# Graph attention as one loop per layer with a running softmax, in place of three stages

## The chip, the cores and the metric

The kernel runs on one core of a Trainium2 chip. The metric is the device time of one execution in microseconds. The core has five engines that run side by side, each through its own instruction queue: TensorE (PE), VectorE (DVE), ScalarE (ACT), GpSimd (POOL) and SyncE (SP). PE writes to eight PSUM banks; everything else lies in SBUF or in DRAM. SP and POOL start the DMAs here, POOL the indirect ones (gathers and scatters by a list of rows). Engines wait for each other only by semaphores.

## The reference

Eight layers, four graph layers and four mixtures of experts, on 3125 nodes of 256 numbers and 50000 edges sorted by destination. The change touches only the third graph layer, a graph attention of two layers with 8 heads of 32:

```python
q = (h @ Wq).reshape(n, H, DK)
k = (h @ Wk).reshape(n, H, DK)
v = (h @ Wv).reshape(n, H, DV)
e = jnp.sum(q[dst] * k[src], axis=-1) / np.sqrt(DK).astype(np.float32)
m = jax.ops.segment_max(e, dst, num_segments=n)
a = jnp.exp(e - m[dst])
z = jax.ops.segment_sum(a, dst, num_segments=n)
alpha = a / (z[dst] + 1e-09)
msg = v[src] * alpha[:, :, None]
agg = jax.ops.segment_sum(msg, dst, num_segments=n).reshape(n, H * DV)
out = agg @ Wo
return _layer_norm(out + h, g, b)
```

## The kernel before

Nodes stand in NT = 25 tiles of 128 rows. The edges are sorted by destination and cut into CHUNKS = 416 chunks of 128, so that all edges of a chunk have their destination in one tile; `chunks.bin` holds each chunk's tile. A step of the attention's loops takes GS = 4 chunks, so there are 104 steps. All matmuls are fp32, which PE runs in two passes: a matmul counts as two in the profile.

`layer2_gnn` runs for each of its two layers: `dense` (q into SBUF, k and v side by side into the DRAM table `pairs`), then three stages, one after the other with a barrier between, and then the division by z, the product with Wo and the layer norm.

`attention_scores`: POOL gathers rows of k and v, 128 rows of 2 KB for each chunk, into a ring `rows` of 16 chunks (L1000). SP writes the v half of each group of 4 chunks to the DRAM buffer `spill` (L1865, 512 KB). DVE builds one-hot matrices of the destination lanes (L1836), PE turns them (L1901), ACT copies them to SBUF (L1921), PE picks with them each edge's q row (L1909). For each chunk PE first loads the number of its tile from SBUF into a register (L1908). DVE multiplies q and k (L1882) and sums over each head (L1888). A slot of the ring comes free when its reduction and its spill are done. A loop over registers (`steps`) repeats a body of four steps.

`attention_weights`: with all scores there, they are turned to lie by head, and DVE runs scans over 3328 columns forward and back (L2069, L2082, L2084) that give each edge the maximum of its destination; small products of 16 columns carry maxima from block to block. ACT takes the exponential, and all is turned back.

`attention_values`: SP reads `spill` back, DVE builds the same one-hots again (L1836) and multiplies v by the weights (L2132), POOL puts the weights beside them as a count column (L2144), PE sums each chunk into the PSUM bank of its tile (L2162, 264 columns), tiles going round over 8 banks. When a tile has ended, ACT copies its bank to `acc` (L2178) and clears it (L2180).

## Time and profile before

| | us |
|---|---|
| median of 3 runs | 7547.13 |
| lowest and highest | 7526.02, 7561.16 |
| span of the profiled execution | 7555.1 |
| scores stage, layers one and two | 743.4, 746.6 |
| weights stage | 63.4, 63.7 |
| values stage | 200.8, 201.4 |

The page gives the profiled execution by its span alone, from the first instruction to the last. Busy time over the whole program is an average over very different stages (PE 67%, DVE 38%, POOL 29%), and says little on the attention. A stretch of time with the busy time of each engine in it says more. "issue" beside idle time means that the engine waited for nothing that the profile shows. The names of some releasers (`home_rows`, `bias`) are those of other stages that used the same semaphore.

### The profile page before, as it was taken

The numbers are of one execution on the slowest core, as the hardware profiler recorded it, in microseconds if no ns is written. First come the engines' busy times: TensorE is split into PE (matmuls) and PEld (weight loads), VectorE is DVE, ScalarE is ACT, GpSimd is POOL, SyncE is SP. The second block draws the span as 40 slices with busy tenths as digits, with TensorE's granted clock in tenths as the row PEclk, the third lists the DMA queues.
The fourth block names the chain that finished last, engine by engine and source line by source line (L and its number), as shares of the span: only waits on it lengthen the run. The fifth ranks groups of instructions, "written<-read, shape, count | busy, mean of one in ns | idle before, by whom it ended". The sixth has DMA issues, their size and how long they took to land. (4 is left out here: it accounts for less than half of the span.)

```text
span 7555.1 us, 86117 instructions
## 1 busy us (share of the span) xinstructions
PE 5066.7 (67%) x21628; PEld 3356.8 (44%) x21677; DVE 2842.8 (38%) x6162; ACT 1117.7 (15%) x2691; POOL 2221.8 (29%) x2417
## 2 busy tenths in 40 slices
PE   3511969659783597755454965554877969898954
PEld 2410547314771256733222843222767844444433
DVE  4260679201323004244445944445943220202052
ACT  2210235000220002210000120000123220101020
POOL 3356010540244401425553215553300410000014
PEclk9999999769796697977776976777988989999966
DMA  0000023223561223637774827675721644243323
GB/s 14 1 1 1 1 93 139 81 66 120 160 199 65 77 90 123 195 122 228 219 218 137 273 86 224 216 222 160 254 67 40 191 153 153 101 139 115 115 69 114
DMA packets 484296, 952.76 MB, mean 126 GB/s; under 512 B 112617, under 2 KB 292436, under 8 KB 481686
## 3 DMA queue, kind: packets, MB, share of 16 engines
q1 hardware_dynamic: 324614, 633.98, 24.9%
q0 software_dynamic: 114208, 281.05, 12.8%
q10 hardware_dynamic: 45296, 35.56, 1.6%
q8 instruction: 88, 1.44, 0.1%
q14 instruction: 90, 0.74, 0.0%
HBM read 733.91 MB, written 216.46 MB: 126 GB/s over the span
## 5 line engine op out<-in xcount | busy, mean ns | idle before, releaser
L1173 PE MATMUL banks<-ring,xn 128*128 128x512 f32 (+1 forms) x3500 | 1443.9, 568 | 397.6 <-issue 276.9
L1173 PEld LDWEIGHTS banks<-ring,xn 128*128 128x128 f32 x3500 | 644.2, 195 | 1198.0 <-issue 1181.4
L1909 PE MATMUL banks<-agg,hotT 128*128 x1664 | 687.0, 519 | 633.6 <-issue 623.9
L1000 POOL DMA_INDIRECT rows<-pairs,idxr x832 | 804.7, 967 | 640.5 <-DVE scores L1888 373.2
L1909 PEld LDWEIGHTS banks<-agg,hotT 128*128 128x128 f32 x1664 | 319.7, 237 | 949.2 <-issue 945.1
L382 POOL DMA_INDIRECT dst_table<-nodes_pay,nodes_row x392 | 380.0, 969 | 817.5 <-DVEq L1147 478.9
L382 POOL DMA_INDIRECT bin_table<-bins_pay,bins_row x392 | 402.3, 1026 | 592.1 <-ACTq L783 206.8
L1882 DVE TENSOR_TENSOR prod<-banks,rows 128x512 f32<-128x512 f32 x416 | 267.9, 686 | 811.3 <-PE banks L1909 640.7
L1643 PE MATMUL banks<-second,hT 128*128 x1544 | 391.6, 393 | 45.4 <-DVE yr L1689 19.3
L1628 PE MATMUL banks<-xT,w1r 128*128 128x128 f32 x3088 | 403.1, 283 | 12.3 <-DVE xT L1681 7.1
L2162 PE MATMUL banks<-msg,hot 128*128 128x264 f32 x1664 | 384.3, 392 | 16.7 <-DVE msg L2132 16.2
L1628 PEld LDWEIGHTS banks<-xT,w1r 128*128 128x128 f32 x3088 | 382.2, 200 | 16.3 <-issue 9.2
L1065 PE MATMUL banks<-spans,lanes 128*128 128x256 f32 x1440 | 332.3, 387 | 74.8 <-DVE spans L1046 62.7
L2162 PEld LDWEIGHTS banks<-msg,hot 128*128 128x128 f32 x1664 | 313.8, 192 | 86.8 <-issue 30.8
L1689 DVE TENSOR_TENSOR yr<-banks,bias 128x256 f32<-128x256 f32 x235 | 99.8, 424 | 650.6 <-PE banks L1643 554.8
L2386 DVE TENSOR_SCALAR yT<-banks,columns 128x512 f32<-128x512 f32 (+1 forms) x42 | 27.1, 687 | 839.5 <-PE banks L2367 839.5
L713 PE MATMUL banks<-places,loT 64*128 64x14 bf16 (+1 forms) x784 | 178.0, 227 | 241.6 <-issue 127.3
L1605 POOL DMA_INDIRECT home_rows<-yr,home x235 | 233.8, 995 | 359.6 <-DVE yr L1689 343.9
L1547 POOL MEMSET second<- 64x8192 f32 x1 | 6.9, 6919 | 1127.7 <-POOLq L131 1127.7
L1661 ACT ACTIVATE hT<-banks,b1T 128x128 f32<-128x128 f32 x772 | 225.0, 369 | 719.9 <-PE banks L1628 531.3
L1065 PEld LDWEIGHTS banks<-spans,lanes 128*128 128x128 f32 x1440 | 266.8, 191 | 141.1 <-issue 108.2
L1921 ACT ACTIVATE hotT<-banks 128x512 f32<-128x512 f32 x208 | 124.2, 597 | 1365.4 <-PE banks L1901 577.4
(355 smaller groups left out, 6931.4 us busy)
## 6 DMA issues: line engine op xcount, KB each, us to landing
ring<-adjacency SPq DMA_DIRECT2D x145, 1280.0 KB
spill<-rows SPq DMA_DIRECT2D x208, 512.0 KB
rows<-spill SPq DMA_DIRECT2D x208, 512.0 KB
w1r<-in_L_ffn_W SPq DMA_DIRECT2D x114, 512.0 KB
adjacency<-strips SPq DMA_DIRECT2D x13, 3200.0 KB
w1r<-in_L_ffn_w SPq DMA_DIRECT2D x65, 512.0 KB
rows<-home_rows SPq DMA_DIRECT2D x35, 640.0 KB
ring<-adjacency SPq DMA_DIRECT2D x25, 640.0 KB
```

The costliest lines, as they stand in the source:

```text
L382: self.nc.gpsimd.indirect_dma_start(self.table, bass.IndirectOffsetOnAxis(ap=self.row[:, c:c + 1], axis=0), self.pay[:, c * W:(c + 1) * W] ...
L713: nc.tensor.matmul(bank, loT[h * L:(h + 1) * L, c % 4, b * P:(b + 1) * P], places[h * L:(h + 1) * L, c * UB + b, :, :].rearrange("p d n -> ...
L1000: nc.gpsimd.indirect_dma_start(rows[:, row, :], None, table, bass.IndirectOffsetOnAxis(ap=idxr[:, at + g:at + g + 1], axis=0))\
L1065: nc.tensor.matmul(K.banks[:, bass.ds((v % 16) * SPAN_S, SPAN_S)], lanes[:, j, q, :], spans[:, j, q, :], start=False, stop=True, skip_grou ...
L1173: last = nc.tensor.matmul(K.ps[2 * (g % 2) + o][:, 0:wd], x[:, t * D + o * P:t * D + (o + 1) * P], ring.buffer[:, n % R, 0:wd // cols, q * ...
L1605: nc.gpsimd.indirect_dma_start(K.home_rows, bass.IndirectOffsetOnAxis(ap=r.home[:, c:c + 1], axis=0), yr[:, c % R, :], None).then_inc(stor ...
L1628: last = nc.tensor.matmul(K.ps[2 + jj % 2][:, h * P:(h + 1) * P], w1r[:, jj, s, h * P:(h + 1) * P], xT[:, jj % 2, s * P:(s + 1) * P], star ...
L1643: last = nc.tensor.matmul(bank, hT[:, jj % 2, h * P:(h + 1) * P], ahead.second[:, bass.ds(e * (nh * D) + h * D, D)], start=(h == 0), stop= ...
L1661: last = nc.scalar.activation(hT[:, j % 2, h * P:(h + 1) * P], K.ps[2 + j % 2][:, h * P:(h + 1) * P], func, bias=b1T[:, bass.ds(e * nh + h ...
L1882: last = nc.vector.tensor_tensor(prod[:, jj % 2, hh * 2 * D:(hh + 1) * 2 * D].rearrange("p (c d) -> p c d", d=D), K.ps[2 + 2 * (jj % 2) + ...
L1909: last = nc.tensor.matmul(K.ps[2 + 2 * (jj % 2) + g // 2][:, g % 2 * D:(g % 2 + 1) * D], hotT[:, jj % 2, g * P:(g + 1) * P], tile_of(q, t) ...
L2162: nc.tensor.matmul(K.banks[:, bass.ds((v % BANKS) * 512, W)], hot[:, j, g, :], msg[:, j, g, :], start=False, stop=True, skip_group_check=T ...
```

## The change

The three stages become one function, `attention`. Its loops run over i from 0 to 111 and are written out, without registers for i. The chunks are taken in 26 waves of 16 (four steps). In step i, gathers, spill, one-hots, queries, products and reductions run as before, for group i. When the four groups of a wave have scores, their 128 columns (16 chunks of 8 heads) are turned, and the maxima are found by scans of 128 columns, with the last maximum carried over from the wave before (`before`, `after`). If a destination goes on from one wave into the next and its maximum rises, its lanes in the PSUM bank are scaled down (`rescale`). SP reads group i - 5 back from `spill` behind the spill of group i, DVE weighs group i - 8 (`weigh`), and PE sums it with one-hots kept for ten groups (`values`). There are two banks for the sums, by turns from tile to tile. After every chunk ACT copies the bank that the next chunk does not use into `acc` and clears it (`keep`), whether a tile ended or not; what is copied too early is overwritten when the tile ends. PE's chunk k waits for the clearing after chunk k - 2. The weight columns are now interleaved, 33 columns a head, and ACT writes them.

To make room, `acc` takes the place of K.x, which is written to DRAM in `find_segments` and read back beside the last layer norm; the reset table is bf16; two buffers serve again as messages. `number_chunks` writes a bit per chunk (the bank) instead of the marks and ends of tiles.

The core of the diff:

```diff
-PER = -(-CHUNKS // BLOCKS)
-SPAN = PER * P
+WAVES = CHUNKS // BLOCKS
+SPAN = WAVES * P
 RUNS = 4
 GS = 4
+WIDE = HEADS * (DH + 1)
...
+        self.parked = nc.dram_tensor("parked", (P, NT * D), FP, kind="Internal").ap()
...
+LAG = 8
+RING = 16
+HOTS = 10
+MSGS = 2
+VALS = 3
+BEHIND = 5
...
+def attention(nc, K, edges, G, q, acc):
+
     S = CHUNKS // GS
-    with stage(nc) as st:
-        idxr = st.sb("idxr", [P, 2 * GR], I32)
-        rows = st.sb("rows", [P, GR, 2 * D])
-        hot = st.sb("hot", [P, 2, GS, P])
+    GW = BLOCKS // GS
+    B = BLOCKS
+    W = WIDE
+    BIN, BANK = edges.chunks.bin, edges.chunks.bank
...
+                n = RING // GS
+                for i in range(S + BEHIND):
+                    if i < S:
+                        j = i % n
+                        sp.wait_ge(gathered[j], 16 * GS * (i // n + 1))
+                        sp.dma_start(K.spill[i, :, :].rearrange("p (c d) -> p c d", d=D),
+                                     rows[:, GS * j:GS * (j + 1), D:2 * D]).then_inc(spilled[j], 16)
+                    g = i - BEHIND
+                    if g >= 0:
+                        sp.wait_ge(spilled[g % n], 16 * (g // n + 1))
+                        if g >= VALS:
+                            sp.wait_ge(weighed, g - VALS + 1)
+                        sp.dma_start(vals[:, g % VALS, :], K.spill[g, :, :]).then_inc(loaded[g % VALS], 16)
...
+                def weigh(g):
+                    v = g // GW
+                    if g >= MSGS:
+                        dve.wait_ge(summed, GS * (g - MSGS + 1))
+                    dve.wait_ge(loaded[g % VALS], 16 * (g // VALS + 1))
+                    dve.wait_ge(weighted, v + 1)
+                    at = g % GW * GS * HEADS
+                    V.tensor_tensor(msg[g % MSGS][:, :, 0:DH],
+                                    vals[:, g % VALS, :].rearrange("p (q d) -> p q d", d=DH),
+                                    weights[:, v % 2, at:at + GS * HEADS].unsqueeze(2).broadcast_to([P, GS * HEADS, DH]),
+                                    ALU.mult).then_inc(weighed, 1)
...
+                def peaks_of_rows(v):
+                    dve.wait_ge(flipped, v + 1)
+                    V.tensor_tensor_scan(peak[:, 0:P], G.reset[:, v, 0:P], flat, -BIG, ALU.add, ALU.max)
+                    link(V.tensor_tensor_scan(peak[:, P:2 * P][:, ::-1], G.reset[:, v, 1:P + 1][:, ::-1], flat[:, ::-1],
+                                              -BIG, ALU.add, ALU.max))
+                    V.tensor_tensor(ends[:, :, :], G.of_block[:, :].unsqueeze(1).broadcast_to([P, 2, B]),
+                                    peak[:, P - 1:P + 1].unsqueeze(2).broadcast_to([P, 2, B]), ALU.mult).then_inc(ended, 1)
...
+                def rescale(v):
+                    k = v * B
+                    b = dve.value_load(BANK[0:1, k:k + 1], min_val=0, max_val=1)
+                    dve.wait_ge(read, v)
+                    dve.wait_ge(summed, k)
+                    dve.wait_ge(zeroed, k - 1)
+                    bank = K.banks[:, bass.ds(b * 512 + 6 * 512, W)].rearrange("p (h d) -> p h d", d=DH + 1)
+                    V.tensor_tensor(bank, bank, lowered[:, :].unsqueeze(2).broadcast_to([P, HEADS, DH + 1]),
+                                    ALU.mult).then_inc(rescaled, 1)
...
+                for i in range(S + LAG):
+                    last, done = full(i - 1), full(i - 2)
+                    if i < S:
+                        if i >= 2:
+                            dve.wait_ge(turned, i - 1)
+                        if i >= HOTS:
+                            dve.wait_ge(summed, GS * (i - HOTS + 1))
+                        one_hot(nc, edges, K, hot[:, i % HOTS, :, :], i).then_inc(onehot, 1)
+                    if i >= LAG:
+                        weigh(i - LAG)
...
+                def values(g, banks, part):
+                    pe.wait_ge(weighed, g + 1)
+                    pe.wait_ge(slotted, g + 1)
+                    for n in part:
+                        k = GS * g + n
+                        if k >= 2:
+                            pe.wait_ge(zeroed, k - 1)
+                        if k and k % B == 0:
+                            pe.wait_ge(rescaled, k // B)
+                        nc.tensor.matmul(K.banks[:, bass.ds(banks[n] * 512 + 6 * 512, W)], hot[:, g % HOTS, n, :],
+                                         K.spare[g % MSGS][:, n * W:(n + 1) * W],
+                                         start=False, stop=True, skip_group_check=True).then_inc(summed, 1)
...
+                    if last is not None:
+                        pe.wait_ge(scored, GW * (last + 1))
+                        if last:
+                            pe.wait_ge(weighted, last)
+                        nc.tensor.transpose(flat, scores[:, last % 2, :], K.ident[:, :]).then_inc(flipped, 1)
...
+                def keep(k, t, b):
+                    act.wait_ge(summed, k + 1)
+                    if k:
+                        act.wait_ge(zeroed, k)
+                    bank = K.banks[:, bass.ds((1 - b) * 512 + 6 * 512, W)]
+                    nc.scalar.activation(tile_of(acc, t, W), bank, ACT.Copy).then_inc(kept, 1)
+                    act.wait_ge(kept, k + 1)
+                    nc.scalar.activation(bank, zeros[:, :], ACT.Copy).then_inc(zeroed, 1)
...
```

In `layer2_gnn` the calls of the three stages become `attention(nc, K, by_dst, G, q, acc)`.

**PE, one step.** Before, in the loop's body: a load of a register stands ahead of every query.

```order
L1901 MATMUL banks<-ident,hot 128x128 x4
L1908 ISA
L1908 TENSOR_LOAD chunks
L1908 ISA x2
L1909 ISA
L1909 MATMUL banks<-agg,hotT 128x256
L1908 ISA
L1908 TENSOR_LOAD chunks
L1908 ISA x2
L1909 ISA
L1909 MATMUL banks<-agg,hotT 128x256
```

After, the step in which a wave has just got all its scores: two loads at its head, each for four chunks, then the wave's turn, the one-hots' turn and the queries.

```order
L2063 TENSOR_LOAD chunks
L2067 TENSOR_LOAD chunks
L2074 MATMUL banks<-ident,scores 128x128
L2080 MATMUL banks<-ident,hot 128x128 x4
L2088 ISA
L2088 MATMUL banks<-agg,hotT 128x256
L2088 ISA
L2088 MATMUL banks<-agg,hotT 128x256
```

Behind the four queries follow the four value matmuls of the group eight steps back (L2054), which stood in a stage of their own.

**ACT, one step.** Before, in the scores stage, ACT had one copy a step:

```order
L1919 REGISTER_ALU
L1921 ACTIVATE hotT<-banks 128x512
L1919 REGISTER_ALU
L1921 ACTIVATE hotT<-banks 128x512
L1919 REGISTER_ALU
```

After, the weight column (L2140), the same copy, and a copy to `acc` (here under the name x) and a clearing after every chunk, four a step:

```order
L2130 TENSOR_LOAD chunks
L2133 TENSOR_LOAD chunks
L2140 ACTIVATE bins_pay<-weights 128x32
L2146 ACTIVATE hotT<-banks 128x512
L2121 ISA x2
L2121 ACTIVATE x<-banks 128x264
L2123 ACTIVATE banks<-zeros 128x264
L2121 ISA x2
L2121 ACTIVATE x<-banks 128x264
L2123 ACTIVATE banks<-zeros 128x264
```

The ring of value matmul, copy and clearing is new in ACT's and PE's step.

**DVE, the long step of a wave.** The softmax of the wave stands between the weighing and the next one-hot:

```order
L1938 TENSOR_TENSOR bins_pay<-vals,weights 128x32x32
L1945 SCALAR_TENSOR_TENSOR peak<-reset,banks 128x128
L1946 SCALAR_TENSOR_TENSOR peak<-reset,banks 128x128
L1948 TENSOR_TENSOR ends<-of_block,peak 128x32
L2022 TENSOR_TENSOR prod<-banks,rows 128x512 x2
L1954 SCALAR_TENSOR_TENSOR before<-through_f,before,banks 8x16
L1956 SCALAR_TENSOR_TENSOR after<-through_r,banks 8x16
L1958 TENSOR_TENSOR past<-before,joint 8x16
L1960 TENSOR_SCALAR risen<-after,before 8x1
L1962 TENSOR_TENSOR past<-after,joint 8x16
L2034 TENSOR_REDUCE scores<-prod 128x32
L1966 TENSOR_TENSOR ends<-banks,of_block 128x32
```

Seven more operations follow before the next step's one-hot, which PE's next transposes wait for.

## Rows read from the trace of the kernel before

**Rows 1.** The page: its first line.
```profile
span 7555.1 us, 86117 instructions
```

**Rows 2.** Stages of layer one, sum of six: us, each engine's busy us, clock, DMA, GB/s.
```profile
3337.10:4080.50 743.40, 402.77 (x1248) 220.78 (x1248) 323.35 (x416) 62.11 (x104) 413.37 (x468) 0.73 0.72 220
4080.50:4143.90 63.40, 11.30 (x60) 10.42 (x60) 48.44 (x64) 8.97 (x26) 0.00 (x0) 0.54 0.00 0
4143.90:4344.70 200.80, 192.14 (x832) 156.65 (x832) 190.10 (x210) 19.64 (x50) 55.27 (x104) 0.97 0.81 272
...
sum 2019.30, PE 1219.20 PEld 778.00 DVE 1123.37 ACT 181.45 POOL 962.43; mean PE 203.20 PEld 129.67 DVE 187.23 ACT 30.24 POOL 160.41
```

**Rows 3.** Groups by line, scores stage of layer one: busy, mean ns, idle before.
```profile
L1000 POOL DMA_INDIRECT rows<-pairs,idxr x416 | 402.6, 968 | 317.7 <-DVE scores L1888 201.4 <-issue 115.9 <-POOL idxr L989 0.4
L1909 PE MATMUL banks<-agg,hotT 128*128 x832 | 342.4, 517 | 320.3 <-issue 313.9 <-DVE prod L1882 2.3 <-ACT hotT L1921 0.9
...
L1882 DVE TENSOR_TENSOR prod<-banks,rows 128x512 f32<-128x512 f32 x208 | 133.9, 686 | 403.9 <-PE banks L1909 325.4 <-DMA bias<-in_L_ffn_b 37.6 <-issue 32.2
L1888 DVE TENSOR_REDUCE scores<-prod 128x1024 f32 (+1 forms) x104 | 126.8, 1220 | 15.5 <-DVE prod L1882 4.2 <-issue 3.3
...
L1836 DVE TENSOR_TENSOR hot<-iota,by_dst_pay 128x512 f32<-128x512 f32 x104 | 71.0, 684 | 4.0 <-PEq L131 3.4 <-PE banks L1901 0.6
```

**Rows 4.** One cycle of the scores stage, columns as in rows 2.
```profile
3637.50:3645.50 8.00, 6.25 (x24) 2.94 (x23) 6.23 (x8) 1.20 (x2) 6.15 (x7) 1.00 0.58 162
3645.50:3661.00 15.50, 3.48 (x11) 1.84 (x10) 3.10 (x4) 0.60 (x1) 9.85 (x12) 0.65 0.89 275
...
3664.00:3666.70 2.70, 2.34 (x11) 1.32 (x10) 2.22 (x4) 0.20 (x1) 0.14 (x1) 1.00 0.00 0
```

**Rows 5.** Instructions in order of time: gathers on POOL, spills on SP.
```profile
3637.52 0.97 POOL L1000 DMA_INDIRECT rows<-pairs,idxr  x1 [8.38 <-DVE scores L1888]
...
3645.12 0.51 SPq L1865 DMA_DIRECT2D spill<-rows  x1
...
3651.19 0.51 SPq L1865 DMA_DIRECT2D spill<-rows  x1
...
3666.56 0.97 POOL L1000 DMA_INDIRECT rows<-pairs,idxr  x1 [8.60 <-DVE scores L1888]
3667.83 0.94 POOL L1000 DMA_INDIRECT rows<-pairs,idxr  x1 [0.31 <-issue]
```

**Rows 6.** The same on DVE, products of two steps in a free stretch.
```profile
3666.51 1.29 DVE L1882 TENSOR_TENSOR prod<-banks,rows 128x512 f32<-128x512 f32 x2 [0.32 <-PE banks L1909]
...
3670.77 1.29 DVE L1882 TENSOR_TENSOR prod<-banks,rows 128x512 f32<-128x512 f32 x2 [0.97 <-PE banks L1909]
```

**Rows 7.** The same on PE and ACT, before and in the slow stretch.
```profile
3643.28 0.69 PE L1909 MATMUL banks<-agg,hotT 128*128 x2 [0.18 <-issue]
...
3651.20 1.22 PE L1909 MATMUL banks<-agg,hotT 128*128 x2 [5.04 <-issue]
...
3654.87 0.60 ACT L1921 ACTIVATE hotT<-banks 128x512 f32<-128x512 f32 x1 [12.03 <-DMA home_rows<-yr,home]
```

**Rows 8.** PE's register loads, scores stage of layer one: ns min/median/max.
```profile
L1908 PEldq TENSOR_LOAD <-chunks x415: 2/302/1398, 3340.5 to 4075.9; - x139
```

**Rows 9.** In order of time, weights stage: a wide and a narrow scan.
```profile
4093.27 7.09 DVE L2069 TENSOR_TENSOR_SCAN peak<-reset,scoresT 128x3328 f32<-128x3328 f32 x1 [0.67 <-PEq L131]
...
4101.14 0.18 DVE L2074 TENSOR_TENSOR_SCAN scan<-through_f,small 8x16 f32<-8x16 f32 x1
```

**Rows 10.** Groups by line, values stage, both layers, columns as in rows 3.
```profile
L2162 PE MATMUL banks<-msg,hot 128*128 128x264 f32 x1664 | 384.3, 392 | 16.7 <-DVE msg L2132 16.2
...
L2132 DVE TENSOR_TENSOR msg<-rows,scores 128x1024 f32<-128x1024 f32 x208 | 254.7, 1225 | 0.0
...
L2180 ACT ACTIVATE banks<-zeros 128x264 f32<-128x264 f32 x50 | 19.7, 395 | 1.6
```

**Rows 11.** DMA queues, 3337.1 to 4080.5, then 4143.9 to 4337: packets, MB, share.
```profile
q0 software_dynamic: 33280, 109.08, 50.1%
q1 hardware_dynamic: 54912, 54.53, 21.5%
q14 instruction: 4, 0.03, 0.0%
...
q1 hardware_dynamic: 14976, 54.53, 84.0%
```

More of the change, by code:

```diff
@@ L160, in __init__ @@
     def __init__(self, st):
[L161 to L163 removed]
+        self.all = st.sb("chunks", [1, 2 * CHUNKS + 1], I32)
+        self.bin, self.bank = self.all[:, 0:CHUNKS], self.all[:, CHUNKS:2 * CHUNKS + 1]
 class Core:
@@ L1848, in attention_scores @@
         hotT = st.sb("hotT", [P, 2, GS * P])
         prod = st.sb("prod", [P, 2, GS * D])
-        gathered = [st.sem(f"gathered{j}") for j in range(4)]
-        spilled = [st.sem(f"spilled{j}") for j in range(4)]
+        msg = [buf[:, 0:GS * W].rearrange("p (q d) -> p q d", d=DH + 1) for buf in K.spare]
+        scores = st.sb("scores", [P, 2, P])
+        weights = st.sb("weights", [P, 2, P])
+        peak = st.sb("peak", [P, 2 * P])
+        over = st.sb("over", [P, P])
+        zeros = st.sb("zeros", [P, W])
@@ L1854, in attention_scores, with full @@
+        scaled, read, rescaled, weighed, slotted, cleared, summed, kept, zeroed = (
+            st.sem(x) for x in ("scaled", "read", "rescaled", "weighed", "slotted", "cleared", "summed", "kept", "zeroed"))
+        def full(i):
+            v = (i - 1) // GW - 1
+            return v if (i - 1) % GW == 0 and 0 <= v < WAVES else None
         with nc.Block() as block:
@@ L1992, in find_segments @@
-        vector_work(nc, *[lambda h=h: nc.vector.tensor_copy(nodes4[:, :, :, h], node) for h in range(HEADS)])
-        turn(nc, K, nodes, lambda o: (nodesT[:, o * P:(o + 1) * P], None))
-        chain, packed, moved = st.sem("chain"), st.sem("packed"), st.sem("moved")
+        nodes = st.sb("nodes", [P, SPAN])
+        nodesT = st.sb("nodesT", [P, WAVES, P])
+        ends = st.sb("ends", [P, 3, WAVES, B])
+        small = st.sb("small", [HEADS, 3, CHUNKS])
+        low = st.sb("low", [P, WAVES])
@@ L2002, in _ @@
+                last.then_inc(moved, 1)
             @block.vector
```

465 lines of the change are left out of this document (243 added, 222 removed).

## The prediction, made before the changed kernel had run

> **What bounds the kernel now.** I read the stage table first [rows 2]. In each of the two layers the attention is three stages in a row: scores 743.4 us, weights 63.4 us, values 200.8 us; with the second layer the six stretches sum to 2019.3 us, so 1009.65 us a layer. Everything else in the program stays as it is but for a parking copy, so the change can move only these.
>
> The values stage is dense: DVE is busy for 190 of 200.8 us and PE for 192. The weights stage is one chain of wide DVE scans with no DMA. The scores stage is odd: no engine is busy for even 60% of it (POOL 413 of 743 us, PE 403, DVE 323), DMA share 0.72. The groups by line [rows 3] put 313.9 us of PE's idle time before the query matmul at "issue", and the product's idle time at PE's banks, so I looked at one cycle of it [rows 4]. POOL starts a burst of gathers at 3637.5 and the next at 3666.6 [rows 5], 29.05 us for 4 steps of 4 chunks. From 3637.5 to 3645.5 PE and DVE run freely; DVE's products are 4.26 us apart in such a stretch [rows 6]. From 3645.5 to 3661 nearly everything stands still but POOL and DMA, whose share is 0.89. The stretch begins when the first spill goes out beside running gathers [rows 5] and ends as the gathers run out. Inside it PE waits 5 us for "issue" before a single query instead of 0.2, and ACT's copy comes 12 us late [rows 7]; PE's register load has a median of 302 ns in the stage and a maximum of 1398 [rows 8]. So gathers and spills together slow PE's and ACT's sequencers, the 16-slot ring fills, POOL stops, DMA drains, and it starts again. I don't know the mechanism; I use its price. A step costs 743.4/104 = 7.15 us against 4.26 free: 2.9 us lost for 15.5/4 = 3.9 us of the mixed stretch, that is 0.74 us for each us of mix.
>
> **Part by part.** S is the new step of 4 chunks, 104 a layer; before, a layer spends 1009.65/104 = 9.71 us on each in all three stages together.
>
> *Removed:* the weights stage (63 us a layer: packing copies, transposes, four scans over 3328 columns at 7.1 us [rows 9], barriers), the values stage's own pass and one of two one-hot builds a step (0.69 us), the count column by POOL.
>
> *DVE a step:* one-hot 0.69, weighing 1.23, product 2 x 0.686, reduction 1.22 = 4.5 us [rows 3, 10]. A wave of 4 steps adds four scans of 128 columns (7091/3328 = 2.13 ns a column, 0.27, plus about 0.1 fixed, since 16 columns take 0.18 [rows 9]): 1.6 us; some eleven small operations of 0.16 to 0.2: 2.0; the bank's rescaling about 0.45 and a register load 0.3; some 14 waits for its own last result at 0.05: 0.7. That is 5.1 us a wave, so 23.1 us for 4 steps, 5.8 a step. Most of it falls in one step, 9 to 10 us long.
>
> *ACT and PE a step:* ACT now copies and clears a bank after every chunk, not after every tile: 832 small activations a layer where 50 ran, 0.39 us busy each [rows 10] and about 0.42 with the hand-over, 3.4 us a step, plus hotT 0.6, the weight column about 0.25 and two register loads 0.6. With two banks PE may be one chunk ahead of it. The ring of one step: PE's two loads 0.7, transposes 0.65, four queries about 1.8, first value matmul 0.46 (384.3 us for 832 executions of two passes [rows 10]), then three matmuls each behind an ACT pair, 2.5: about 6.1 us. In the wave's long step PE's next transposes wait for a one-hot that stands behind DVE's softmax chain, so that step takes what DVE takes, about 9.7. Free step F = (3 x 6.1 + 9.7)/4 = 7.0 us. Bounds: 5.8 (DVE's busy time alone, round trips hidden) and 8.4 (every round trip of the wave in the open). I take 7.0. POOL (4 x 1.25 us and an index copy, 5.2) stays below it.
>
> *DMA a step:* gathers 0.501 x 743.4/104 = 3.58 us of all 16 engines, spill 0.215 x 743.4/104 = 1.54, reading back 0.84 x 193.1/104 = 1.56 [rows 11]: 6.68. The readback used to stand in its own stage; now it is in the same loop. At the mixed stretch's share of 0.89 this needs 7.5 us; at the spacing of spills in it (6.1 us for 5.12 us of work, 0.84) 8.0. So DMA alone forbids a step below 7.5. The Trainium skill, "DMA: Bandwidth & Descriptors" (section Where 436 GB/s comes from), puts the limit of HBM traffic at about 358 GB/s for a core; by it the 2.10 MB of a step would need an estimated 5.9 us and DMA would not bind. The trace moved 275 GB/s in the mixed stretch at a share of 0.89 [rows 4], which speaks for the larger figure.
>
> *The mix in the new loop.* A compute step longer than POOL's 5.2 us leaves the ring full: one group's gathers go out per step, when its product is done. From the first gather of a burst to its spill are 7.5 us [rows 5]; spill and readback then take 1.54 + 1.56. So a group's traffic lasts 10.6 us, and mix M = 10.6 - S a step overlaps with the next group's. S = F + 0.74 M gives S = (7.0 + 7.84)/1.74 = 8.53 us, M about 2.1.
>
> *The sum.* A layer: memsets before the first one-hot 8, 104 x 8.53 = 887, eight last steps with values alone 8 x 4.5 = 36, end 3: 934 us against 1009.65, so -75.6, twice -151. Parking K.x (3.3 MB written, 6.25 times a spill of 0.52 MB and its 1.54 us, so 9.6 us, at the end of find_segments beside short DVE work) I put at +10, between 0 and 20; reading it back lies beside the layer norm. Two or three small operations in number_chunks are under 1. The page gives the profiled execution's span, 7555.1 us [rows 1], 8 above the median of 7547.1 and within the three runs. 7555 - 151 + 10 = 7414, less those 8: 7406. With F at its bounds S is 7.84 or 9.33, the time 7263 or 7572. I say 7405.
>
> **Rivals.** *A, the slow sequencers don't come back.* PE reads 4 register values by one load, two loads a step against four, and bursts are one group long, so backlog never builds; in the values stage, read-only traffic at 0.84 share never slowed PE [rows 10, 11]. Then DMA binds at 7.5: 7406 - 208 x 1.03 = 7192; with DMA better than I think, S = 7.0 and 7088. Against it: total traffic at S = 7.5 is 280 GB/s, as much as in the bad stretch.
>
> *B, the mix covers most of a step: slower.* Spill and readback take 3.1 us alone and about twice that beside gathers, as the spill does today; ACT, which had one instruction a step to be late with, now has about twenty and is in the ring. With M = 5, S = 7.0 + 3.7 = 10.7, time 7406 + 208 x 2.17 = 7857. It decides from S = (1009.65 - 5 - 47)/104 = 9.2 (5 is half the parking, 47 the layer's two ends). For it: PE and ACT are the two that suffer, and the change puts the clearing there. Against: a longer step itself thins the traffic.
>
> *C, code.* The loops are written out (PE from 3491 rows to 7124, ACT from 1729 to 4953 in program order), so instructions stream in behind gathers; today's stage fetched 5 blocks [rows 11]. Some 33 more blocks of 256 rows, up to 5 us each if not covered: +165, to about 7570. The Trainium skill, "Runtime: NRT & Kernel Launch" (section Instruction fetch mechanics), says that crossing a block in straight code is mostly hidden; no run yet shows it here.
>
> **Chances and range.** Forecast (S 7.8 to 9.3) 0.47, A 0.20, B 0.28, C 0.05. Likeliest 7405, its own range 7263 to 7572. Eight in ten: 7130 to 7800, which cuts A's low end and the upper half of B. 0.5%, 38 us, is about what a measurement can tell: faster (below 7509) is A and four fifths of the forecast and a little of C, 0.61; within, 0.08; slower, B and the forecast's tail, 0.31.
>
> **What would show it.** Stage length over 104 near 8.5 us; DMA share near 0.78 (at 7.2 or less B, at 0.9 A); PE's "issue" idle before the query L2088 in the changed kernel, much below 314 us a layer if A, well above if B; ACT about 60% busy with copy and clear; every fourth step about 3.5 us longer than the rest. Idle time of the product for want of gathered rows would prove me wrong, as would any move outside the attention above 15 us.

## The result

The changed kernel takes 7515.37 us (median of 6 runs, 7510.04 to 7522.79) against 7557.62 for the kernel before (6 runs, 7526.02 to 7571.39): ratio 0.9944, 95% interval 0.9927 to 0.996. The forecast was 7405 in a range of 7130 to 7800. The sign and the range held. Against the median of 7547 known then, 142 us of gain were forecast; 42 came.

This is one group of runs on one chip. The experiments came in groups, each beside the kernel before on the same chip, and the chips fell into two kinds: on one the kernel before takes 7479 to 7558 us (chips A), on the other 6413 to 6417 (chips B). On a chip B the same change is 4.9% slower, and that is the larger finding.

### The profile page after: what moved, and what is told of

Read it like the earlier page. It is cut to its first block and busy times, and to the rows that moved or that the text cites. A ratio compares the mean times of both kernels' runs of the same rounds, so it can differ in the third digit from the quotient of the medians.

```text
span 7512.8 us, 86978 instructions
## 1 busy us (share of the span) xinstructions
PE 5151.3 (69%) x21926; PEld 3443.6 (46%) x21975; DVE 2817.6 (38%) x6705; ACT 1775.8 (24%) x4567; POOL 2144.2 (29%) x2209
## 5 line engine op out<-in xcount | busy, mean ns | idle before, releaser
L1007 POOL DMA_INDIRECT rows<-pairs,idxr x832 | 866.3, 1041 | 912.2 <-DVE prod L2022 637.0
L2088 PE MATMUL banks<-agg,hotT 128*128 x1664 | 527.6, 474 | 0.6 <-issue 0.6
L2121 ACT ACTIVATE x<-banks x832 | 324.6, 390 | 638.3 <-PE banks L2054 410.8
L2088 PEld LDWEIGHTS banks<-agg,hotT 128*128 128x128 f32 x1664 | 393.6, 249 | 66.4 <-issue 1.4
L2054 PE MATMUL banks<-nodes_pay,hot 128*128 128x264 f32 x832 | 304.0, 478 | 168.6 <-ACT banks L2123 81.9
L2054 PE MATMUL banks<-bins_pay,hot 128*128 128x264 f32 x832 | 284.0, 449 | 169.9 <-ACT banks L2123 95.7
L2080 PE MATMUL banks<-ident,hot 128*128 128x128 f32 x832 | 173.6, 345 | 307.6 <-DVE hot L1845 260.9
L1698 DVE TENSOR_TENSOR bins_pay<-banks,bias 128x256 f32<-128x256 f32 x235 | 99.8, 425 | 645.7 <-PE banks L1652 552.6
L1614 POOL DMA_INDIRECT home_rows<-bins_pay,home x235 | 233.1, 992 | 361.1 <-DVE bins_pay L1698 344.0
L2123 ACT ACTIVATE banks<-zeros 128x264 f32 x832 | 328.0, 394 | 26.3
```

Of the source, the lines that this page charges most:

```text
L1007: nc.gpsimd.indirect_dma_start(rows[:, row, :], None, table, bass.IndirectOffsetOnAxis(ap=idxr[:, at + g:at + g + 1], axis=0))\
L1614: nc.gpsimd.indirect_dma_start(K.home_rows, bass.IndirectOffsetOnAxis(ap=r.home[:, c:c + 1], axis=0), yr[:, c % R, :], None).then_inc(stor ...
L2054: nc.tensor.matmul(K.banks[:, bass.ds(banks[n] * 512 + 6 * 512, W)], hot[:, g % HOTS, n, :], K.spare[g % MSGS][:, n * W:(n + 1) * W], star ...
L2088: query = nc.tensor.matmul(K.ps[1 + 2 * (c % 2) + n // 2][:, n % 2 * D:(n % 2 + 1) * D], hotT[:, c % 2, n * P:(n + 1) * P], tile_of(q, t), ...
L2121: nc.scalar.activation(tile_of(acc, t, W), bank, ACT.Copy).then_inc(kept, 1)
L2123: nc.scalar.activation(bank, zeros[:, :], ACT.Copy).then_inc(zeroed, 1)
```

## The profile after

The page's first rows, and then stretches of layer one: find_segments' end, the attention stage, and one wave of four steps in it (columns: stretch, us, busy us of PE, PE's loads, DVE, ACT, POOL, then granted clock, DMA share, GB/s).

```profile
span 7512.8 us, 86978 instructions
...
PE 5151.3 (69%) x21926; PEld 3443.6 (46%) x21975; DVE 2817.6 (38%) x6705; ACT 1775.8 (24%) x4567; POOL 2144.2 (29%) x2209
```

```profile
3337.10:3346.40 9.30, 4.77 (x15) 2.35 (x13) 3.34 (x9) 0.03 (x1) 0.11 (x1) 0.93 0.23 85
3346.40:4330.20 983.80, 647.54 (x2286) 431.93 (x2286) 548.01 (x962) 420.19 (x1118) 443.32 (x468) 0.83 0.71 222
3752.66:3788.89 36.23, 24.54 (x88) 16.54 (x88) 20.82 (x38) 16.21 (x43) 17.97 (x19) 0.86 0.73 230
```

The three stages of [rows 2], 1007.6 us, have become one of 983.8; layer two went from 1011.7 to 981.3, and the parking copy moved the start by 9.3. That is -23.8 - 30.4 + 9.3 = -45, where the spans differ by -42: the rest of the program differs by 3 us in sum. No engine is busy for more than 66% of the new stage.

The groups by line (busy, mean ns, idle before and its releasers) that answer to [rows 3, 10]:

```profile
L2088 PE MATMUL banks<-agg,hotT 128*128 x1664 | 527.6, 474 | 0.6 <-issue 0.6
L2080 PE MATMUL banks<-ident,hot 128*128 128x128 f32 x832 | 173.6, 345 | 307.6 <-DVE hot L1845 260.9 <-issue 46.7
...
L1945 DVE TENSOR_TENSOR_SCAN peak<-reset,banks 128x128 f32<-128x128 bf16 x52 | 21.9, 421 | 279.6 <-issue 149.0 <-PE banks L2074 130.7
...
L2121 ACT ACTIVATE x<-banks x832 | 324.6, 390 | 638.3 <-PE banks L2054 410.8 <-ACT banks L2123 126.8 <-issue 93.7
```

The slow stretch is gone: the queries, which stood 633.6 us at "issue" and others over both layers (313.9 of them at issue in layer one alone [rows 3]), now stand 0.6. In its place PE waits 261 us for a one-hot, and ACT 411 us for value matmuls. DVE is idle for 280 us before the scan of the turned scores; the profile puts 131 of them to PE's turning and 149 to "issue", but in the same kernel on a chip B all 266 to PE (e14 below). So each of the three engines waits for another one, in a circle. One wave in order of time on DVE shows how:

```profile
3754.82 0.68 DVE L1845 TENSOR_TENSOR hot<-iota,by_dst_pay 128x512 f32<-128x512 f32 x1
3760.65 0.17 DVE L1982 TENSOR_SCALAR lowered<-banks 128x8 f32<-128x8 f32 x1 [4.01 <-PE banks L2094]
3765.40 0.44 DVE L1991 TENSOR_TENSOR banks<-banks,lowered 128x264 f32 x1 [2.10 <-ACT banks L2123]
3765.75 0.68 DVE L1845 TENSOR_TENSOR hot<-iota,by_dst_pay 128x512 f32<-128x512 f32 x1
3769.94 0.68 DVE L1845 TENSOR_TENSOR hot<-iota,by_dst_pay 128x512 f32<-128x512 f32 x1
3774.13 0.73 DVE L1845 TENSOR_TENSOR hot<-iota,by_dst_pay 128x512 f32<-128x512 f32 x1
3780.63 0.42 DVE L1945 TENSOR_TENSOR_SCAN peak<-reset,banks 128x128 f32<-128x128 bf16 x1 [4.64 <-issue]
3788.89 0.19 DVE L1966 TENSOR_TENSOR ends<-banks,of_block 128x32 f32<-128x32 f32 x1 [3.25 <-issue]
3791.04 0.68 DVE L1845 TENSOR_TENSOR hot<-iota,by_dst_pay 128x512 f32<-128x512 f32 x1
```

From the one-hot at 3754.82 to that at 3791.04 are four steps in 36.2 us, 9.06 each. DVE's one-hots come 10.9, 4.2, 4.2 and 16.9 us apart; what stands before the long gaps is first the rescaling (L1982, L1991), then the softmax of the next wave (L1945, L1966), each with waits for the other engines of 2 to 5 us. PE, on the same wave:

```profile
3755.56 1.11 PE L2080 MATMUL banks<-ident,hot 128*128 128x128 f32 x4 [2.93 <-DVE hot L1845]
3756.47 3.62 PE L2088 MATMUL banks<-agg,hotT 128*128 x8
3760.02 0.59 PE L2094 MATMUL banks<-head_fade,head_hot 8*128 8x8 f32 x2
3766.49 0.66 PE L2080 MATMUL banks<-ident,hot 128*128 128x128 f32 x4 [1.64 <-issue]
3766.99 1.89 PE L2088 MATMUL banks<-agg,hotT 128*128 x8
3772.64 0.63 PE L2080 MATMUL banks<-ident,hot 128*128 128x128 f32 x4 [0.20 <-issue]
3773.11 1.89 PE L2088 MATMUL banks<-agg,hotT 128*128 x8
3780.39 1.06 PE L2080 MATMUL banks<-ident,hot 128*128 128x128 f32 x4
```

Its transposes are 10.9, 6.2, 7.8 and (to 3791.78) 11.4 us apart: two long steps in a wave, not one. And after the wait of 2.93 us for the one-hot the same four queries take 3.62 us instead of 1.89; the granted clock is 0.50 in that stretch (3755.56 to 3760.02), the 1.2 GHz level, and 1.00, the 2.4 GHz level, from 3766.49 to 3768.90. The other waves do the same: of 206 groups of four queries in both layers, the 56 behind a wait of 2 us or more took 2.8 to 3.6 us each, and of the 91 behind a wait under 1 us 76 took 1.89. The product that the rescaling needs (L2094) stands behind the queries.

The tail of the stage, where only values are left, shows ACT's ring with nothing around it:

```profile
4314.36 0.26 ACT L2140 ACTIVATE bins_pay<-weights 128x32 f32<-128x32 f32 x1 [0.97 <-issue]
4316.36 0.39 ACT L2121 ACTIVATE x<-banks  x1 [1.74 <-PE banks L2054]
4316.78 0.39 ACT L2123 ACTIVATE banks<-zeros 128x264 f32 x1
4317.51 0.39 ACT L2121 ACTIVATE x<-banks  x1 [0.34 <-ACT banks L2123]
...
4321.89 0.26 ACT L2140 ACTIVATE nodes_pay<-weights 128x32 f32<-128x32 f32 x1 [0.96 <-issue]
```

A copy is 1.15 us behind the last (0.42 to the clear, 0.73 to the next copy), not 0.84, and a step takes 7.53 us, not 4.5. What makes the 0.73 is in ACT's own queue:

```profile
L2121 ACTq FUSED_REGOPS  x1664: 37/64/113, 3409.8 to 5464.8; - x185
L2121 ACTq MOVE  x832: 29/29/29, 3409.7 to 5464.6; - x167
```

The copy's place in `acc` depends on the tile, so three register instructions (29, 85 and 37 ns here) stand between `keep`'s waits and the copy, and with the hand-overs between them they fill the 0.34 us of idle time. The clear uses the address that is there already and follows its copy with 0.03 us idle. The place is known from the step's loads, so the registers could be worked out ahead of the wait. No run tried it.

## The experiments

Ratios are to the kernel before on the same chip. "Attention" is layer one's stretch from clearing x (L1998) to the first operation behind the stage, some 3 us less than the stage as a whole.

**Is it the single loads?** e1 to e3 (chip A, before 7551.9 us).

```diff
-  for g in range(GS):
-      t = pe.value_load(edges.chunks.bin[0:1, bass.ds(c * GS + g, 1)], ...)
+  _, tiles = nc.values_load_multi_w_load_instructions(
+      edges.chunks.bin[0:1, bass.ds(GS * c, GS)], [mybir.EngineType.PE], ...)
+  for g, t in enumerate(tiles):
```

> The kernel before, with one edit in its scores stage: TensorE fetches the four tile numbers of a step with one register load of four values, as the changed kernel does, instead of one load ahead of each of the four query products. Theory LOADS (the single loads are what made TensorE's instructions come late in the slow stretches): the long gaps ahead of the queries go, a step falls from 7.15 us to between 5.2 and 6.1 us, so the six-stage sum falls by 2 x 104 x (1.05 to 1.95), and the time is 7150 to 7340 us. Theory MIX (gathers together with spill writes slow every instruction of TensorE's sequencer, as the prediction took it): only three of the slow stretch's loads go; the gaps ahead of the queries stay, and the time is 7450 to 7560 us.

7431.0 us, ratio 0.9848 (0.9825 to 0.9871): between the ranges of the two theories. The queries of e1, then its products:

```profile
L1911 PE MATMUL banks<-agg,hotT 128*128 x1664 | 525.8, 472 | 99.2 <-issue 81.1 <-ACT hotT L1923 13.9
```

```profile
L1882 DVE TENSOR_TENSOR prod<-banks,rows 128x512 f32<-128x512 f32 x416 | 267.4, 685 | 687.1 <-DMA bias<-in_L_ffn_b 565.4 <-PE banks L1911 71.0 <-issue 31.6
```

PE's idle time at issue went from 624 to 81 us. DVE's wait for a transfer grew by 465 (565 against 100, in 56 waits of some 10 us), so that DVE's whole idle time before the products fell by 124, about the gain. A step fell only from 7.15 to 680.9/104 = 6.55 us: behind the loads' stall stood a wait for gathered rows.

e2 writes a quarter of each spill and reads that quarter four times.

```diff
-  sp.dma_start(K.spill[i, :, :]..., rows[:, GS * j:GS * (j + 1), D:2 * D])
+  sp.dma_start(K.spill[i, :, 0:D]..., rows[:, GS * j:GS * j + 1, D:2 * D])
```

> The kernel before, with the spill cut to a quarter: of each step's four chunks of values only the first is written to memory, and the values stage reads that one four times (so three quarters of the values are left out and replaced by the first chunk's). Loads, gathers, products and register loads are as before. Theory MIX: with a quarter of the bytes beside the gathers the slow stretch shrinks to a quarter or goes, a scores step falls to 4.9 to 5.8 us, time 7150 to 7380 us. Theory LOADS (single register loads are the cause whatever the DMA queues do): the step stays at 7.0 to 7.2 us and the time at 7480 to 7570 us.

7551.23 us, ratio 1.0003 (0.9991 to 1.0016); the queries' idle time at issue is 594.6 us. So the spill's bytes beside the gathers, on which 0.74 M of the forecast stood, aren't the cause. A kernel without any spill transfer was not run.

e3 gives the changed kernel the four single loads back.

```diff
-  for n, t in enumerate(tiles):
+  for n in range(GS):
+      t = pe.value_load(BIN[0:1, c * GS + n:c * GS + n + 1], ...)
```

> The changed kernel, with one edit: TensorE again fetches a tile number with a load of its own ahead of each of the four query products. Theory LOADS: the late issue returns, the gap ahead of a query goes from 0 to 0.5 us or more, a step grows by about 2 us, 2 x 104 x 2 = 420 us, and the time is 7800 to 8000 us. Theory MIX, with the mix gone because loads and spills are now spread over the whole step: four loads of about 0.3 us in place of one of 0.33, some of it beside other work: 0 to 0.9 us a step, 7515 to 7700 us.

7678.41 us, ratio 1.0171 (1.0148 to 1.0194), 163 us above the changed kernel and in the range of theory MIX. The queries grew from 528 to 672 us busy and wait 109. Most of that is the loads' own price of about 0.3 us. The long gaps hardly come back (88 us at issue), so single loads alone don't make the slow stretch either.

e8 (chip A, before 7479.1) is e1 and e2 together.

> The kernel before with both earlier edits: one register load of four values a step on TensorE, and the spill cut to a quarter (the values stage reads the first chunk's values four times, the other three chunks' are left out). With the one load alone VectorE and ScalarE waited 565 and 146 us more for DMA, at 224 GB/s. Theory DMA (once the loads are gone, the bytes of gathers and spill bound a step at about 6.6 us): three eighths of the bytes less gives 104 x 2 x (0.8 to 2.2) us, time 6975 to 7265 us. Theory GATHER (the eight indirect transfers of a refill, 1.25 us apart, bound it at whatever size the spill has): 7350 to 7435 us.

7389.93 us, ratio 0.9876 (0.9857 to 0.9896), no better than e1: what DVE waits for there (454 us) isn't the spill's bytes. This is the range of theory GATHER.

**What fills the changed kernel's step?** e4 (chip A, with e1 to e3) builds the one-hots one step ahead.

```diff
-HOTS = 10
+HOTS = 11
-  if i >= 2:
-      dve.wait_ge(turned, i - 1)
-  one_hot(nc, edges, K, hot[:, i % HOTS, :, :], i)
+  for h in ((0, 1) if i == 0 else (i + 1,)):
+      one_hot(nc, edges, K, hot[:, h % HOTS, :, :], h)
```

> The changed kernel, with the one-hots built one step ahead (eleven buffers instead of ten, the one-hot of step i + 1 at the head of VectorE's step i, and no wait for the transposes). Theory HOT (TensorE's wait for a one-hot that stands in VectorE's queue behind a wave's serial chain is what makes two of four steps 11 us long; that wait measured 261 us over both layers): 150 to 260 us come back, time 7255 to 7365 us. Theory CHAIN (the two long steps are the serial chain scan, product, scan, product, scan itself; the one-hot only stands at its end, and the same time passes in the next wait of VectorE): under 60 us come back, time 7455 to 7515 us.

7309.68 us, ratio 0.9681 (0.9658 to 0.9703): 206 us back, as HOT has it. PE's wait fell from 260.9 to 27.0:

```profile
L2080 PE MATMUL banks<-ident,hot 128*128 128x128 f32 x832 | 163.5, 330 | 90.4 <-issue 58.0 <-DVE hot L1845 27.0 <-ACT hotT L2146 5.1
```

e5 to e7 (chip A, with e8). ACT's second load, of four values from an offset of one (L2133), took 920 ns; e5 copies the table once to `later` and loads from a multiple of four.

```diff
+  V.tensor_copy(later[:, :], BANK[0:1, 1:CHUNKS + 1])
-  BANK[0:1, GS * g + 1:GS * (g + 1) + 1]
+  later[0:1, GS * g:GS * (g + 1)]
```

> The changed kernel, with one edit: the table of bank bits that ScalarE reads one chunk ahead (four values from an offset of one) is copied once a layer into a table of its own, so that the second register load of a step starts at a multiple of four as the first does. In the changed kernel that load took 920 ns, the one beside it 309 ns. Theory ACT (ScalarE's ring of keep pairs, loads and hotT copy sets the plain steps): 0.6 us of 2 x 104 steps, 60 to 125 us come back, time 7390 to 7455 us. Theory CHAIN (the two serial steps of a wave set the time, and ScalarE waits in the others for TensorE): under 30 us, 7485 to 7520 us.

7418.33 us, ratio 0.9922 (0.9902 to 0.9942). The load took 309 ns. By the ratio that is 17 us less than the changed kernel's 0.9944, within the intervals nothing; by attention 46 us a layer (981.0 to 935.3), but on another chip, on which the kernel before is 79 us faster too. Left open between the two theories.

> The changed kernel with both edits: one-hots one step ahead, and the aligned table for ScalarE. With the one-hots ahead the plain steps measured 7.3 us from ScalarE's copy to the next (3724.92 to 3732.23 us), in which VectorE is busy for 4.2: theory ACT expects the whole 0.6 us in at least two of four steps, 60 to 125 us below 7310, time 7185 to 7250 us. Theory CHAIN: 7280 to 7312 us.

7228.27 us, ratio 0.9664 (0.9646 to 0.9682); its interval overlaps e4's, so the same stays open there.

e7 leaves out the rescaling between waves (scale, its read, L1991).

> The changed kernel without the rescaling between waves: the product of the fade (scale), VectorE's read of it and its multiplication of the bank are left out, so a tile's sums keep the scale of the wave in which they were made (this part of the softmax is left out of the result). Theory TWO LONG STEPS (the rescaling makes the second long step of a wave: 177 us of VectorE's waits for the product, 95 us for ScalarE's clear, and the next one-hot behind them): that step falls from 11.4 us to between 6 and 8, 2 x 25 waves x (3.4 to 5.4) = 170 to 270 us, time 7245 to 7345 us. Theory BODY (its 50 multiplications of 0.44 us and reads of 0.17 us are all that it costs, 30 us): 7450 to 7500 us.

7376.46 us, ratio 0.9862 (0.9843 to 0.9881): 62 us less than the changed kernel by the ratio, 65 a layer or 130 in all by attention (981.0 to 915.8, on another chip). Either way it is more than the bodies (30) and less than the 170 of the other theory. DVE no longer waits 177 us for the product of the fade and 95 for the clear behind it, but it now waits 196 before the weighing. That line in the changed kernel, and then in e7:

```profile
L1938 DVE TENSOR_TENSOR bins_pay<-vals,weights 128x1024 f32<-128x1024 f32 x104 | 126.5, 1217 | 23.5 <-ACT weights L2158 14.1 <-PE banks L2054 9.4
```

```profile
L1938 DVE TENSOR_TENSOR bins_pay<-vals,weights 128x1024 f32<-128x1024 f32 x104 | 126.9, 1220 | 195.7 <-PE banks L2048 101.2 <-ACT weights L2146 78.7 <-issue 15.7
```

Taking one link out of the circle moves most of the wait to the next.

**The column of weights and the clears.** e9 to e12 (chip B, before 6417.24). e9:

```diff
+  V.tensor_copy(msg[g % MSGS][:, :, DH], weights[:, v % 2, at:at + GS * HEADS])
-  nc.scalar.activation(msg[g % MSGS][:, :, DH], weights[:, v % 2, at:at + GS * HEADS], ACT.Copy)
```

> The changed kernel, with one edit: the column of weights of each message (slot, 0.26 us on ScalarE) is written by VectorE just ahead of its product of values and weights, so ScalarE's step is register loads, hotT copy and four keep pairs, and TensorE's values no longer wait for ScalarE's queue. In the tail of eight steps the changed kernel's step measured 7.53 us: 4.87 us of keep pairs, and 1.54 us from slot to TensorE's first values and on to the first keep, and 0.96 + 0.2 us of loads. Theory VALUES RING (slot to values to keep is a serial ring in each step): the tail steps fall to about 6.0 us, which alone is 24 us, and the steps ahead of them by up to as much: ratio to the kernel before 0.970 to 0.985. Theory QUERIES (ahead of the tail TensorE's queries and VectorE's chain hide it): the tail alone, ratio 0.988 to 0.993.

6642.41 us, ratio 1.0348 (1.033 to 1.0365). Every expectation of this group took chips to be alike, so its ratios don't hold here, and only differences between runs on chips B say something. Against the changed kernel on another chip B (e14) it is 81 us less, inside what theory VALUES RING would give there.

> The changed kernel with the three edits together: one-hots one step ahead, the aligned table for ScalarE, and the column of weights written by VectorE. The first two measured a ratio of 0.966 to the kernel before. Theory VALUES RING: 0.3 to 0.9 us a step more comes back, ratio 0.940 to 0.958. Theory QUERIES: the tail alone, ratio 0.959 to 0.965.

6388.58 us, ratio 0.996 (0.9946 to 0.9974): 335 us less than e14.

> The three edits, and TensorE's product of the fade (scale, two passes, 0.35 us) issued ahead of the transposes and the four queries in place of behind them. It is 50 steps in which VectorE's read of it came 0.4 to 0.8 us late and the multiplication of the bank 1.6 to 2.3 us late. Theory SCALE (the rescaling is late because its product stands behind queries at half clock, 3.1 to 3.5 us): 50 x (0.5 to 2) = 25 to 100 us below the three edits, 0.003 to 0.013 of the ratio. Theory CLEAR (the rescaling waits for ScalarE's clears of the wave's last chunks in any case, 95 us in the changed kernel): within 0.003 of it, or a little slower, since TensorE now waits for VectorE's shift before it may turn the one-hots.

6493.88 us, ratio 1.0123 (1.0106 to 1.0139), 105 us slower than e10. The product of the fade now waits 122.9 us for DVE's chain, with the transposes and queries behind it, and the rescaling still waits for ACT's clears, 237 us instead of 100. This is theory CLEAR, and worse than it said.

e12 leaves the clears out of the changed kernel; who waited for a clear waits for the copy.

```diff
-  act.wait_ge(kept, k + 1)
-  nc.scalar.activation(bank, zeros[:, :], ACT.Copy).then_inc(zeroed, 1)
```

> The changed kernel without the clearing of a bank after each copy (half of each keep pair: 0.39 us busy and 0.34 us until the next copy may start; the banks go on summing across tiles, so the sums are not a tile's own). Theory KEEP (832 keep pairs of 1.16 us in place of the 0.84 forecast are part of what sets a step): 4 x 0.73 us less on ScalarE's ring, of which 0.5 to 2 us a step come back, time ratio 0.937 to 0.98. Theory CHAIN (the two serial steps of a wave and the one-hot behind them set it): ratio 0.985 to 0.995.

6378.61 us, ratio 0.9939 (0.9923 to 0.9956): 345 us less than e14, which is theory KEEP; that the ratio falls into theory CHAIN's range is the chip's doing. DVE's wait for the turned scores, in e14 and then in e12:

```profile
L1945 DVE TENSOR_TENSOR_SCAN peak<-reset,banks 128x128 f32<-128x128 bf16 x52 | 21.8, 420 | 265.6 <-PE banks L2074 265.6
```

```profile
L1945 DVE TENSOR_TENSOR_SCAN peak<-reset,banks 128x128 f32<-128x128 bf16 x52 | 21.8, 419 | 99.6 <-PE banks L2074 99.6
```

No clear is near that scan. But in PE's queue the turning of the scores stands behind the value matmuls of the step before, each of which waits for a cleared bank: 236 us of waits for ACT in e14, 97 in e12. So DVE's chain starts late when ACT is late.

**Both kernels on one chip B** (before 6413.01 us):

> The kernel before once more, profiled on the chip of this group, so that its stages stand beside the next three's. The last four runs fell on a chip where this kernel takes 6417 us and not 7480 to 7557, and where the waits of TensorE that the profile gives to issue are mostly gone (276 us of them in the adjacency products of the first profile, none of them there in the changed kernels' profiles). Theory ISSUE (the slow stretches of the scores stage are of the same kind, and so belong to the chip and not to the kernel): on a chip of about 6400 us the scores stage of this kernel takes 4.3 to 6.0 us a step with queries' issue idle under 100 us; on one of about 7500 us 7.15 with 620 us. Theory LOADS (the slow stretch is the price of four single loads anywhere): 7 us and 600 us on either.

> The changed kernel once more, on the same chip. Theory ISSUE: on a chip of about 7500 us a ratio of 0.993 to 0.996 as first measured; on a chip of about 6400 us the change has nothing of the slow stretch to gain and keeps its two long steps, so it is slower, ratio 1.01 to 1.04. Theory LOADS: 0.99 to 1.00 on either.

e13: 6414.27 us, and its scores stage takes 5.3 us a step, as theory ISSUE has it. e14: 6723.8 us, ratio 1.0491 (1.0473 to 1.0508), slower still than the 1.01 to 1.04 of that theory. The three stages of e13:

```profile
2607.90:3160.00 552.10, 385.80 (x1248) 213.65 (x1248) 322.53 (x416) 62.11 (x104) 416.62 (x468) 0.85 0.93 296
3160.00:3222.50 62.50, 11.49 (x60) 10.61 (x60) 48.02 (x63) 8.62 (x25) 0.00 (x0) 0.54 0.00 0
3222.50:3423.70 201.20, 192.19 (x832) 156.75 (x832) 190.52 (x213) 20.01 (x53) 56.25 (x104) 0.97 0.80 271
```

and the one of e14:

```profile
2607.20:3575.20 968.00, 646.01 (x2286) 429.58 (x2286) 547.95 (x963) 420.13 (x1118) 444.94 (x468) 0.83 0.71 226
```

Against [rows 2], weights and values are the same on both kinds (62.5 and 201.2); the scores stage is 552 us instead of 743, 5.3 us a step, close to POOL's eight gathers and one index copy for two steps (8 x 1.25 + 0.5); POOL's gathers wait for DVE and transfers for 24 us in both layers, and the products wait 298 us for gathered rows. The changed stage takes nearly the same on both kinds (968 and 984 us), but with the two edits attention takes 804 us on a chip B (e15) and 841 on a chip A (e6). So the changed stage takes 152 us more than e13's three a layer, and on chips A 24 to 30 less. The queries' idle time at issue is 211 us in e13, more than the 100 that theory ISSUE allowed, and 624 in the first profile. PE's own queue instructions at the load say what kind of stall it is; e13, then the kernel before on chip A (ns min/median/max):

```profile
L1908 PEldq FUSED_REGOPS  x1632: 46/151/163, 2610.9 to 4118.5; - x182
...
L1908 PEldq SEQ_ASSERT  x832: 18/18/18, 2611.1 to 4118.7; - x167
```

```profile
L1908 PEldq FUSED_REGOPS  x1632: 2/151/1396, 3340.1 to 5242.5; - x182
...
L1908 PEldq SEQ_ASSERT  x832: 2/18/1411, 3340.3 to 5242.7; - x167
```

Register instructions that touch no memory take up to 1.4 us on chip A and at most 163 ns on chip B, while the loads themselves are alike (median 302 and 307 ns). A single load brings three such instructions along (1632 and 832 for 832 loads). But they are slow only there. Of the register instructions ahead of the queries in e1 and in the changed kernel, both on chips A, none is, and with the single loads back in the changed kernel (e3) a few are again:

```profile
L1911 PEldq FUSED_REGOPS  x832: 46/46/63, 3343.1 to 5111.4; - x167
```

```profile
L2088 PEldq FUSED_REGOPS  x832: 46/46/57, 3357.6 to 5404.1; - x167
```

```profile
L2084 PEldq FUSED_REGOPS  x832: 3/151/1422, 3353.3 to 5567.5; - x167
```

In layer one 5 of the 1244 FUSED_REGOPS in PE's queue take more than 0.4 us in e3, and 139 of 1257 in the scores stage of the first profile. So the stall needs a chip A, the single loads, and something more of the old stage, which no run isolates. ACT's queue was not slow: its register instructions in that stage took 35 ns every time.

```profile
L1919 ACTq ALU_OP  x150: 35/35/35, 3376.0 to 5230.3; - x150
```

Chips A have a second slowness, which e1 lays bare: DVE's waits for gathered rows are some 10 us long there (565 us in 56 waits), and 3 us in e13 (298 in 99). And the adjacency products, which no edit touches, stand 277 us at issue in the first profile and 0 in e13.

> One-hots one step ahead and the aligned table, on the same chip as the changed kernel. The sum of what they gave: attention of a layer 844 and 849 us against 984 and 981, but on another chip. Theory HOT: 230 to 290 us below the changed kernel on this chip as well, whichever it is. Theory CHIP (half of the difference was the chip's): 100 to 200 us.

6403.66 us, ratio 0.9987 (0.9978 to 0.9997), 320 us less than e14 and more than either theory had.

> The same, and the column of weights written by VectorE, on the same chip. Attention of a layer took 791 and 807 us with it, on the fast chip. Theory VALUES RING: 40 to 110 us below the two edits. Theory QUERIES: the tail alone, 5 to 25 us below them.

6373.58 us, ratio 0.9937 (0.992 to 0.9953): 30 us more, between the two.

> The changed kernel with the three edits (one-hots ahead, aligned table, column of weights by VectorE) once more, beside the next run. On two chips on which the kernel before takes 6413 and 6417 us it measured ratios of 0.9937 and 0.996; the two edits without the column measured 0.9987 there and 0.9664 on a chip of 7479 us. Theory CHIP (a stage of this order takes the same time on either kind of chip, and only the kernel before loses its slow stretches): ratio 0.955 to 0.965 if the chip is of the slow kind, 0.993 to 0.997 if not. Theory SAME: the ratio on a slow chip is near 0.995 too.

A chip B again: 6382.38 us, ratio 0.9948 (0.9931 to 0.9964). The three edits never ran on a chip A.

> The three edits and no clearing of the banks (half of each keep pair left out; the banks go on summing across tiles, so the sums are not a tile's own). In the changed kernel alone the missing clears took attention of a layer from 968 to 797 us, with chips of one kind. Theory KEEP (ScalarE's keep pairs and TensorE's wait for the cleared bank are still the longest ring with the three edits in): 0.8 to 1.7 us of each of 2 x 104 steps, 165 to 350 us below e17. Theory BODY (the three edits and the missing clears share one slack, and what is left is bodies of TensorE and VectorE and gathers at 5.3 us a step): 40 to 165 us below e17.

6173.74 us, ratio 0.9626 (0.9609 to 0.9642), 209 us below e17, in the range of theory KEEP: the keep pairs are still in the longest ring. Attention is 703 us, with DMA share 0.92 at 310 GB/s in its stretch:

```profile
2608.00:3314.20 706.20, 552.11 (x2286) 374.31 (x2286) 553.59 (x1068) 240.02 (x598) 455.39 (x467) 0.94 0.92 310
```

The versions to use: the two edits (one-hots ahead, aligned table), 3.4% faster than the kernel before on a chip A and about equal on a chip B; the three edits (also the column of weights by DVE), 0.4 to 0.6% faster in three groups on chips B.

## Why the prediction was off

- *The slow stretch and its 0.74 M.* The price was read rightly, its cause wrongly: the stretch stays with a quarter of the spill's bytes (e2), PE's part of it nearly goes with one load in place of four though the step falls only to 6.55 us (e1), and on chips B the stage takes 552 us in place of 743. ACT's queue was not slowed, as the prediction took it, only made to wait. The forecast carried 1.53 us a step of it into the new loop; the queries' 0.6 us at issue say it is zero. Rival A had this right and its time (7192) wrong.
- *F, the free step: the step that failed.* It was forecast at 7.0 between bounds of 5.8 and 8.4, and is (983.8 - 8 - 60 - 3)/104 = 8.78, with 60 for the tail. Two errors lie in it. First, a wave has two long steps and not one: the softmax, and a step later the rescaling, behind both of which the next one-hot stands. The forecast was three steps of 6.1 and one of 9.7; the wave above has 10.9, 6.2, 7.8 and 11.4, and the second long step is 4.8 of the 8.3 us more. Second, three keeps were put at 0.84 each, from a copy and a clear 0.42 apart [rows 10]. In the old values stage a clear is followed by a copy more than 6 us later, so nothing there could show the 0.73 us from a clear to the next copy; that alone is 0.9 us a step. The runs price these in us of the whole time: one-hots ahead 206 (e4, chips A), clears 345 (e12) and 209 with the three edits in (e18, chips B). They overlap, so they don't add.
- *The tail*, 4.5 a step: 7.53, which is 24 us a layer. It is the same ring.
- *The sum.* 1.53 too much and 1.78 too little a step make 26 us a layer; with the tail 50, twice 100, which is the gap between -151 and -54. That the time fell inside the range at all is luck: two errors of 160 and 185 us a layer cancel. And that it fell rather than rose is the chip's: on a chip B, where the old stage has little of the slow stretch, the same kernel rises by 4.9%.
- *The signs.* A DMA share of 0.72 or less was to show rival B and the missing idle time at issue rival A; 0.71 and 0.6 us came, one for each: 6.7 us of DMA work in a step of 9 is such a share without any slow stretch. ACT was to be busy about 60% with copy and clear; it is 43% with all its work.
- *DMA at least 7.5 us a step:* not so on a chip B, where e18's stage takes 706/104 = 6.8 us, tail and ends included. On a chip A nothing ran fast enough to say.
- *Right:* the parking (+10, measured 9.3), next to nothing else moved, and the products of the new stage never waited for gathered rows but at each layer's first step. Rival C's cost did not come, as its chance of 0.05 had it: the program fetched 130 and 158 packets of instructions instead of 88 and 90, and no wait follows them; its 5 us a block showed nowhere. The Trainium skill, "Runtime: NRT & Kernel Launch" (section Instruction fetch mechanics), calls crossings in straight code mostly hidden; e14's stage agrees, with 0.6 us at issue before the queries.

## What to carry over

In a loop of several engines write each ring down with every hand-over measured between two instructions that really follow each other, and look at what stands behind each wait in the queue: a producer with slack (here the one-hots) belongs ahead of the serial chain, not behind it, and so, though no run here tried it, does register work. When a stage's loss is at "issue", run the kernel before on a second chip before building on it, since a change that gains only from that loss can lose everywhere else. And when one wait is taken away in a circle of engines that all wait, expect a part of its sum, and find the ring by leaving work out (the clears) sooner than by reading who waits.

## What was not expected of the hardware

- Two kinds of chip, 7.5 and 6.4 ms for one program. On the slower kind single register instructions of PE's queue take up to 1.4 us beside the single loads of the old stage (at most 63 ns ahead of the queries of e1 on such a chip), and waits for gathered rows are some 10 us long. What makes them so was not found.
- ACT's clear starts 0.42 us behind the copy that it waits for, but the next copy 0.73 us behind the clear, because three register instructions stand behind that wait.
- A register load of four values takes 309 ns at an offset that is a multiple of four and 920 ns one beyond (e5 against the changed kernel, medians).
- After a wait of 2.9 us PE's four queries ran at a granted clock of 0.50 and took 3.62 us, against 1.89 at 1.00: in this loop a wait of PE is paid for twice.
